# Causal self-attention inside a decoder layer: the narrow blocks' score steps taken in pairs

## The reference

```python
def _L0_attn_ref(x, Wq, bq, Wk, bk, Wv, bv, Wo, bo, rel_key):   # 16 heads of 8, P = 256
    q, k, v = split_heads(x @ Wq + bq), split_heads(x @ Wk + bk), split_heads(x @ Wv + bv)
    scores = jnp.einsum('bhid,bhjd->bhij', q, k)
    rel = jnp.einsum('bhid,pd->bhip', q, rel_key)
    rel_idx = jnp.clip(j - i + p - 1, 0, p - 1)
    bias = jnp.take_along_axis(rel, jnp.broadcast_to(rel_idx[None, None], (b, h, s, s)), axis=3)
    logits = jnp.where(j <= i, (scores + bias) * scale, -jnp.inf)
    out = jnp.einsum('bhij,bhjd->bhid', jax.nn.softmax(logits, axis=-1), v)
    return out.transpose(0, 2, 1, 3).reshape(b, s, e) @ Wo + bo
```

## Time and profile before

| | |
|---|---|
| median of 3 runs | 498.36 us |
| profiled execution | 497.16 us, of which the span of the core 495.4 us |
| TensorE matmul busy | 449.7 us, 91% |
| VectorE busy | 335.2 us, 68% |
| ScalarE busy | 267.2 us, 54% |
| GpSimd busy | 162.0 us, 33% |
| self-attention loop | about 38 to 338 us of the span |

### The profile page before, as it was taken

How to read it: one execution, slowest core, us unless ns; L and a number is a source line. 1 busy time by engine, 2 the same in 40 slices (tenths; PEclk the granted TensorE clock), 3 DMA queues, 4 the chain that set the end, 5 groups by cost and what they waited for, 6 DMA issues and landing times.

```text
span 495.4 us, 17255 instructions
## 1 busy us (share of the span) xinstructions
PE 449.7 (91%) x7304; PEld 274.2 (55%) x7304; DVE 335.2 (68%) x684; ACT 267.2 (54%) x811; POOL 162.0 (33%) x95
## 2 busy tenths in 40 slices
PE   0879999999999799999799999998898989999997
PEld 0554655655655555655565665564454434666765
DVE  5555886657977667885857887766667587466633
ACT  2546556756456446556535655554454556554653
POOL 7147383333350952360752422084300000001000
PEclk9999999999999799999889999999889899999999
DMA  8211000000100000000000000000000004503151
GB/s 287 66 70 46 26 3 24 24 18 8 26 24 1 24 10 17 26 24 2 24 3 24 3 3 3 3 4 2 2 0 1 1 0 172 171 23 141 53 176 38
DMA packets 17465, 19.49 MB, mean 39 GB/s; under 512 B 1659, under 2 KB 14575, under 8 KB 17263
## 3 DMA queue, kind: packets, MB, share of 16 engines
q1 hardware_dynamic: 17391, 18.41, 11.5%
HBM read 16.17 MB, written 2.16 MB: 37 GB/s over the span
## 4 chain that ended last, share of the span: by engine, by line
PE 70%; DVE 17%; issue 5%; ACT 5%; DMA 2%; POOL 1%; DVEq 0%; SPq 0%; ACTq 0%; POOLq 0%
PE psT L1432 15%; PE psS L1403 14%; PE psS L1413 8%; PE psOM L1372 8%; PE psT L1792 5%; PE psS L1775 4%; DVE neg_max L1058 3%; DVE x_max L1033 2%; PE psS L1622 2%; PE psOM L1513 2%; ACT prob L663 2%; PE psT L1513 2%; PE psOM L1649 1%; DVE prob L1278 1%; PE psOM L1460 1%
## 5 line engine op out<-in xcount | busy, mean ns | idle before, releaser
L663 ACT ACTIVATE prob<-psS,neg_max 128x208 f32<-128x208 f32 (+23 forms) x256 | 121.2, 479 | 74.3 <-DVE neg_max L1058 74.1
L1058 DVE TENSOR_REDUCE neg_max<-psS 128x2 f32<-128x672 f32 (+23 forms) x128 | 91.7, 717 | 64.8 <-PE psS L1413 63.8
L445 POOL TENSOR_TENSOR stat<-stat,pack_a_sb 128x4 f32<-128x4 f32 (+2 forms) x16 | 54.7, 3416 | 169.9 <-DVE stat L876 123.0
L1432 PE MATMUL psT<-pack_a_sb,prob 128*128 128x128 f32 (+4 forms) x640 | 99.2, 287 | 6.3 <-DVE pt_even L1014 3.3
L1432 PEld LDWEIGHTS psT<-pack_a_sb,prob 128*128 128x128 f32 (+4 forms) x640 | 65.1, 133 | 48.5 <-issue 31.4
L1403 PE MATMUL psS<-k_v,q_both 64*32 64x336 f32 (+23 forms) x2048 | 88.5, 403 | 2.6 <-ACT prob L663 1.3
L1413 PE MATMUL psS<-rel_shifted,q_both 36*32 36x268 f32 (+16 forms) x2048 | 71.8, 338 | 0.0
L479 POOL TENSOR_TENSOR q_both<-qT,pack_a_sb 128x1024 f32<-128x1024 f32 x16 | 31.6, 1973 | 85.4 <-PE psS L1413 82.9
L1413 PEld LDWEIGHTS psS<-rel_shifted,q_both 36*32 36x32 f32 x2048 | 37.4, 110 | 24.7 <-issue 17.5
L663 ACT ACTIVATION_READ_ACCUMULATOR prob<-psS,neg_max 128x1 f32 x256 | 50.5, 197 | 0.0
L1792 PEld LDWEIGHTS psT<-pack_b_sb,prob 128*128 128x128 f32 x288 | 36.1, 191 | 18.6 <-DVE prob L1278 11.7
(11 more groups left out here) (172 smaller groups left out, 597.7 us busy)
## 6 DMA issues: line engine op xcount, KB each, us to landing
q_rep<-q_scratch SPq DMA_DIRECT2D x128, 32.0 KB
k_v<-w_scratch SPq DMA_DIRECT2D x8, 512.0 KB, 5.9
q_both<-w_scratch SPq DMA_DIRECT2D x8, 512.0 KB, 6.6
pack_b_sb<-pack_b_dram SPq DMA_DIRECT2D x1, 1641.5 KB, 9.7
X<-x_dram SPq DMA_DIRECT2D x4, 256.0 KB, 5.3
q_scratch<-qT SPq DMA_DIRECT2D x4, 256.0 KB, 2.0
out_dram<-X SPq DMA_DIRECT2D x4, 256.0 KB, 2.3
pack_a_sb<-pack_a_dram SPq DMA_DIRECT2D x1, 535.0 KB, 4.4
```

What stands on the lines that cost most here:

```text
L445: nc.gpsimd.tensor_tensor(st[:, 5, 0:groups], st[:, 2, 0:groups], ca["root"][0:parts, 0:groups], ALU.pow).then_inc(seeded, 1)
L663: ins = nc.scalar.activation(prob[:, s % 4, half, 0:wide], psS[:, 2 * (s % 2) + half, 0:wide], ACT.Exp, bias=neg_max[:, s % 2, half:half + 1],
L1058: v.tensor_reduce(neg_max[:, s % 2], psS[:, 2 * (s % 2):2 * (s % 2) + 2, 0:wide], AX_X, ALU.max, negate=True).then_inc(max_ready, 1)
L1432: ins = nc.tensor.transpose(psT[0:w, k % 2, at:at + T], prob[:, s % 4, half, j * T:j * T + w], ident)
```

## The change

In the narrow blocks the steps u = 2 and 3, 4 and 5, 6 and 7 are taken as pairs. The two steps of a pair write their scores side by side into the same pair of banks, the odd one 256 columns further (`bank_at`), both as wide as the odd step needs (`read_width`: 16 more columns at u = 4 and u = 6). One reduction takes the maxima of both steps, for which `neg_max` has four slots. Then come the exponentials of both, and on TensorE the transposes of the two steps before and, up to u = 5, two quarters of the attention. `scores_read` is waited for by pairs of banks (`fill_of`, `first_step`). The first two steps of a narrow block and all steps of the wide blocks stay as they were. The loops of the four engines still go over single steps, and the work between the steps keeps its place by `u`.

```diff
+        def in_pair(g, u):
+            return ORDER[g % TB] < 2 and u >= 2
+        def read_width(g, u):
+            return width(ORDER[g % TB], u | 1 if in_pair(g, u) else u)
...
+        def bank_at(s):
+            g, u = divmod(s, BS)
+            return 2 * (fill_of[s] % 2), 256 * (u % 2) if in_pair(g, u) else 0
...
+            def exponentials(s):
+                act.wait_ge(max_ready, fill_of[s] + 1)
...
             for s in range(ALL_STEPS):
                 if s >= 2:
                     copy_units(s - 2)
...
+                if not in_pair(g, u):
+                    exponentials(s)
+                elif u % 2 == 0:
+                    exponentials(s)
+                    exponentials(s + 1)
                 if g and u == 5:
                     copy_inverses(g - 1)
...
+            def maxima_of_pair(s):
+                bank, at = bank_at(s)
+                dve.wait_ge(scores_ready, s + 2)
+                v.tensor_reduce(neg_max[:, s % 4:s % 4 + 2, :].rearrange("p s b -> p b s"),
+                                psS[:, bank:bank + 2, :].rearrange("p b (s j) -> p b s j", s=2)
+                                [:, :, :, 0:read_width(*divmod(s, BS))],
+                                AX_X, ALU.max, negate=True).then_inc(max_ready, 1)
...
+                if not in_pair(g, u):
+                    maxima(s)
+                    if s >= 2:
+                        copy_units(s - 2)
+                elif u % 2 == 0:
+                    maxima_of_pair(s)
                     copy_units(s - 2)
+                    copy_units(s - 1)
...
-                pe.wait_ge(scores_read, PRO + s - 1)
+                if fill_of[s] > 1:
+                    pe.wait_ge(scores_read, PRO + first_step[fill_of[s] - 1])
...
-                scores(s)
-                if s >= 2:
+                if not in_pair(g, u):
+                    scores(s)
+                    if s >= 2:
+                        transpose_weights(s - 2)
+                    if g and 2 <= u <= 5:
+                        attend_block(g - 1, u - 2)
+                elif u % 2 == 0:
+                    scores(s)
+                    scores(s + 1)
                     transpose_weights(s - 2)
-                if g and 2 <= u <= 5:
-                    attend_block(g - 1, u - 2)
+                    transpose_weights(s - 1)
+                    if u <= 5:
+                        attend_block(g - 1, u - 2)
+                        attend_block(g - 1, u - 1)
```

More of the change, by code:

```diff
@@ L258, in width, with pair_of_banks @@
             return (blk * BS + (5 if u in (2, 3) else u + 1)) * QG
+        def in_pair(g, u):
+            return ORDER[g % TB] < 2 and u >= 2
+        def read_width(g, u):
+            return width(ORDER[g % TB], u | 1 if in_pair(g, u) else u)
+        def pair_of_banks():
+            fills, firsts = [], []
+            for s in range(ALL_STEPS):
+                g, u = divmod(s, BS)
+                if not (in_pair(g, u) and u % 2):
+                    firsts.append(s)
+                fills.append(len(firsts) - 1)
+            return fills, firsts
+        fill_of, first_step = pair_of_banks()
+        def bank_at(s):
+            g, u = divmod(s, BS)
+            return 2 * (fill_of[s] % 2), 256 * (u % 2) if in_pair(g, u) else 0
         def units(blk):
@@ L649, in copy_heads_tile @@
                                      ACT.Identity, scale=cb["ln_g"], bias=cb["q_b"]).then_inc(piece_read, 1)
[L651 removed]
+            def exponentials(s):
                 g, u = divmod(s, BS)
[L653 to L657 removed]
+                wide = width(ORDER[g % TB], u)
+                bank, at = bank_at(s)
+                act.wait_ge(max_ready, fill_of[s] + 1)
                 if s >= 4:
@@ L662, in _ @@
                 for half in range(2):
-                    ins = nc.scalar.activation(prob[:, s % 4, half, 0:wide], psS[:, 2 * (s % 2) + half, 0:wide],
-                                               ACT.Exp, bias=neg_max[:, s % 2, half:half + 1],
+                    ins = nc.scalar.activation(prob[:, s % 4, half, 0:wide], psS[:, bank + half, at:at + wide],
+                                               ACT.Exp, bias=neg_max[:, s % 4, half:half + 1],
                                                accum_out=row_sum[:, g % 2, 2 * u + half:2 * u + half + 1])
                 ins.then_inc(scores_read, 1)
+            for s in range(ALL_STEPS):
+                g, u = divmod(s, BS)
+                b, n = divmod(g, TB)
+                if s >= 2:
[5 more added lines that the diff above has]
+                    exponentials(s + 1)
                 if g and u == 5:
@@ L1391, in scores @@
                 blk = ORDER[n]
-                wide = width(blk, u)
+                wide = read_width(g, u)
+                bank, at = bank_at(s)
                 if u == 0:
@@ L1402, in scores @@
                         rows = slice(HALF_ROWS * half, HALF_ROWS * (half + 1))
-                        mm(psS[32 * c:32 * c + 32, 2 * (s % 2) + half, 0:wide],
+                        mm(psS[32 * c:32 * c + 32, bank + half, at:at + wide],
                            q_blk[rows, g % 2, q0:q0 + QT, :].rearrange("p i h -> p (i h)"),
@@ L1412, in scores @@
                         rows = slice(HALF_ROWS * half, HALF_ROWS * half + QT * HD + QT)
-                        ins = mm(psS[32 * c:32 * c + 32, 2 * (s % 2) + half, lo:wide],
+                        ins = mm(psS[32 * c:32 * c + 32, bank + half, at + lo:at + wide],
                                  q_rel[rows, g % 2, q0:q0 + QT, :].rearrange("p i h -> p (i h)"),
```

16 lines of the change are left out of this document (9 added, 7 removed).

## The result

The changed kernel took 533.39 us (median of 4 runs, 527.79 to 536.96) against 498.36: slower by the factor 1.069, 95% interval 1.061 to 1.077. The factor leaves out the slowest of the four executions, which counts as slow. I had forecast 518, at most 525. The profiled execution took 533.06 us.

A forecast was written before the change was run, and what follows sets the result against it. The loop was taken as bound by TensorE's list in order. Block terms of 11.5 us plus 9.0 for clock falls gave 20.5 on the profiled 497.16, 517.7; predicted 518 us, range 507 to 525.

The forecast's parts named there:

- the third of block 5: Block 5's step from line 834's end to the normed tile: 1.04 us as before, tile at 137.7, piece waiting 1.0.
- the port's hold for line 834: Layer norm of blocks 5, 9, 13: GpSimd's bias add holds VectorE's line 834, making the norm 1.0 us later.
- The projection behind both steps' exponentials: Blocks 5, 9, 13: the u = 7 projection waits for a copy behind both steps' exponentials; +3.1, +4.1, +3.8 us.
- `khT`: Block 3: the projection waits for the copy of u = 6's key piece; 2.1 us idle, +1.7 us.
- The head piece: Blocks 9 and 13: the u = 3 head piece waits for the u = 2 piece's copy; 0.85 us more.
- The clock: TensorE's granted clock falls once after each new idle stretch in blocks 5, 9, 13; 9.0 us.
- The change of kind: TensorE pays 0.11 us when the kind of matmul changes; pairs save 64 changes, 7.0 us.
- The rule on overlapping drain and fill: Rival on TensorE: changes of kind are free since drain overlaps the next fill, merging saves nothing; 525 us, 8%.
- The clock did not hold: Rival on TensorE's waits: the granted clock does not fall after them; 509 us, 13%.
- the copies did not come in time: Rival in blocks 5, 9, 13 and 3: VectorE and ScalarE run ahead, copies reach TensorE in time; 499 to 500, 5%.
- the merging is far from 0.43 us at each change: Rival on TensorE: each change of kind saves more; 0.43 us makes up the cost, 0.5 gives 493 us; 4%.
- The sign that I gave for being wrong: Block 5's projection starting less than 1.5 us after the piece, or the loop not over 10 us longer.

The follow-up runs named there:

- e1: The changed kernel with GpSimd's query builds and key mask held until VectorE has written the normed tile; 521.13 us, ratio 1.050.
- e3: The changed kernel with the layer norm's variance computed at u = 3, ahead of the maximum of u = 4 and 5; 508.87 us, ratio 1.026.
- e13: The kernel before with two unread matmuls inside each of its two long TensorE waits, in blocks 7 and 11; 492.89 us, ratio 0.989.
- e2: As e1, with GpSimd's bias add also held until the normed tile is written; 515.85 us, ratio 1.037.
- e14: e7 with the same matmuls as e13 in the waits of blocks 7 and 11; 489.59 us, ratio 0.986.
- e7: The changed kernel with pairs only where no piece, head or projection stands behind them; 494.09 us, ratio 0.995.
- e9: e3 with two unread 512-column matmuls behind the piece of blocks 5, 9 and 13; 503.29 us, ratio 1.012.
- e4: The changed kernel with six unread 512-column matmuls ahead of the piece in blocks 5, 9 and 13; 534.01 us, ratio 1.075.
- e6: e3 with nine unread 512-column matmuls behind the piece of blocks 5, 9 and 13; 517.59 us, ratio 1.042.

## Why the forecast was wrong, point by point

- **The step that failed** is the third of block 5: "From there to the start of line 990 before: 136.24 - 135.20 = 1.04." It carried the rest of the norm's chain over at the durations of before. I had named the port's hold for line 834 alone, and had not asked what GpSimd would be doing behind the bias add once the scores of u = 7 came ahead of the piece. It was 139.28 (138.05 + 1.23) to 146.37, 7.1 us. The piece's waits are 6.4, 6.4 and 4.4 us longer than forecast (no key mask in block 13), the projection's 0.7 or more shorter, and 15.1 us were missed in the three blocks. With the builds out of the way (e1) the three lose 10.0 us, where I had forecast 11.0.
- **The mechanism was right.** The projection behind both steps' exponentials: forecast 3.4 us idle, 2.7 in the changed kernel and 2.9 once the builds are out of the way (e1). `khT`: 2.1 forecast, 1.99. The head piece 0.85, 0.76. The maximum over two steps costs as a plain one of as many elements: 1.21 against 1.23.
- **The clock** was forecast at three falls of 3.0 us. A fall costs 2.6 to 3.2 us when the wait before it is short (e3, e13), but blocks 6, 10 and 14 lost 11.8 us to three behind the long waits, of which the last two lasted over 10 us of work each. How long the clock stays down is explained by nothing that I ran: the first, behind a wait as long, lasted 3.9 us of work, and in e2 it stayed down for 13.7 us behind a wait of 0.96.
- **The change of kind** was forecast at 0.11 us at 64 places, 7.0 us; the spread was wrong, and the sum was not borne out. In tile 1 the pair u = 2 and 3 takes 4.05 us where two single steps took 4.50 (125.00 to 129.50): 0.45, so 0.15 each. In tile 0, block 7, nothing (e14). In blocks 3 and 5 the -0.1 and 0.0 of e7 and e14 say that a pair's gain there runs into the wait behind it. At the full clock twelve pairs, for which 0.11 gives 4.0 us, brought 0.7 (e14 against e13); e7's loop is 3.0 shorter than that of the kernel before, but with the clock low in other places.
- **The rule on overlapping drain and fill** (the Trainium skill, "TensorE: Matmul & The Clock Gate", Part 2, "Step-by-step: what each phase is for") would make merging worth nothing: the trace agrees for tile 0 (0.0 us for three pairs, the stall aside) and not for tile 1 (0.45 us for one). The port's rule (the Trainium skill, "SBUF — State Buffer", "SBUF: two separate sides") is what e1 shows (1.88, 2.46 and 2.72 us beside the builds, 0.16, 0.16 and 0.69 without them), and I had applied it to one instruction where it held for four.
- **Rivals.** The clock did not hold, the copies did not come in time, and the merging is far from 0.43 us at each change. None of the four had the GpSimd builds in it; the 5% for what I don't see did. The sign that I gave for being wrong (a projection less than 1.5 us behind its piece) did not come; the time was out of the range on the side where I had looked least.

## What to carry to other kernels

When an instruction is moved ahead of others on the engine that sets the pace, list who is released by it elsewhere, and see which shared port those then keep: a chain of VectorE instructions of 1.2 us in all (0.16 three times and 0.69) took 8.4 beside GpSimd's long ones. Here the producer could be moved more cheaply than the consumer could wait: the variance one step up was worth 24 us by the medians (533.4 to 508.9), 21 by the factors to the kernel before. And a wait of TensorE can cost twice, once by itself and once by the clock behind it. The second part came back with two matmuls, of no use otherwise, in each wait: 4.7 us for the kernel before with nothing else changed. The pairs themselves brought little where nothing waits: 0.7 us of the loop at the full clock.

## What the runs showed of the chip that I had not expected

- A VectorE instruction held by GpSimd is held for one whole GpSimd instruction and again at the next: 1.23, 1.88, 2.46 and 2.72 us for work of 0.16 to 0.69.
- Waits of the same 2.35 us were followed by a fall of the granted clock to 0.50 (1.2 GHz) in blocks 9 and 13 of e3 and by none in block 5. With 1.7 us of them filled (e9) there was none in all three.
- One and the same wait, 1.99 us for `khT`, brought no fall in the changed kernel, nor in e1, e3, e4 and e6, but in e9's profile the clock is at 0.50 from 106 to 113 us and block 4 is 2.7 us longer, and in e2's from 106 to 110 us, block 4 1.1 us longer.
- A float32 matmul of 512 columns stands in the trace as two records and takes 0.86 us (nine in 7.9 us, e6).
